# Attention over 32 heads: TensorE's program without its loop, and four steps of the other engines in another order

## The chip, the cores and the metric

One core of a Trainium2 chip runs the whole program. The metric is the device time of one execution in microseconds (us). The core has five engines with instruction queues of their own, which only semaphores bring together: TensorE (PE, with its weight loads PEld), VectorE (DVE), ScalarE (ACT), GpSimd (POOL) and SyncE (SP), which issues nearly all the DMA transfers of this part.

## What is computed

Two sequences of 2048 tokens of width 512 go through one decoder layer: self-attention with 16 heads of width 64 and a relative position bias, attention to a short context, and a feed-forward part in which 512 chosen tokens get a second, heavier network. The change touches the self-attention alone:

```python
q, k, v = (proj(Wq), proj(Wk), proj(Wv))
scores = jnp.einsum('bhqd,bhkd->bhqk', q, k)
bias = rel_bias[_relative_position_buckets(S)]
scores = scores + bias.transpose(2, 0, 1)[None]
attn = jax.nn.softmax(scores, axis=-1)
ctx = jnp.einsum('bhqk,bhkd->bhqd', attn, v)
```

## The kernel before

The 2 x 16 heads are numbered n = 0 to 31 and worked one after the other; `head(n, k, side)` exists on each engine (POOL, SP, PE, ACT, DVE) and `side` alternates between two sets of buffers. Heads -2 and -1 are only preparation. On PE, ACT, DVE and POOL the helper `heads` writes heads -2, -1, 0 and 29, 30, 31 out and runs heads 1 to 28 in a hardware loop (`Fori`) of 14 rounds with two heads each; SP has loops of its own.

Scores are kept transposed, with keys on the partitions. A head has 32 steps: `qb` (0 or 1) is the half of 1024 queries and `kt` (0 to 15) the tile of 128 keys. Two steps make a group, so a head has 16 groups g. In each group:

- PE (line 610, `largest`) computes two tiles of 128 queries by 512 keys for the row maxima, twice (`pair` 0 and 1), both times into the same two PSUM banks. DVE (line 939) reduces them to maxima. PE starts the next one only when DVE has finished the last (`max_done`). From group 3 on these maxima are those of head n+1.
- PE (line 629, `scores`) computes two steps of scores of head n from the operands in `stacks`. DVE (line 956, `near`) adds the bias near the diagonal, ACT (lines 814 and 817, `exp`) takes the exponential into `probs`, a ring of four steps, and POOL (line 354) adds it into `acc`.
- PE (line 641, `value`) multiplies the probabilities of the group before by V.
- In groups 2, 6, 10 and 14 PE also projects queries and keys of head n+2 (line 590, `project`, block tb = 0 to 3). ACT takes them out, and DVE makes the low parts: `queries_low` (962), `step` (969) in groups 3, 7, 11, 15, and `step_lo` (975) in groups 4, 8, 12 and in group 0 of the next head.

At the end of a half, `sum_of` (PE, line 651) adds up `acc` into PSUM bank PB, which it shares with the projection. ACT copies it to `sums` (`sums_out`, line 794). SP's `divisors` spreads it over partitions with four DMAs (line 431), DVE takes the reciprocal (`reciprocals`, line 982, placed by `RECIP_GROUPS`), and SP writes it to memory and reads it back broadcast (lines 436 and 439). POOL multiplies it in (`context`, line 329, placed by `CONTEXT_STEPS`), and SP's `store_ctx` (line 446) writes the result to memory.

SP works its queue in order. In head n it issues: `fill` of head n+1 (lines 416 to 425: copies of q and k into `stacks`, 12 transfers; it waits until all scores of head n-1 are done, because they read that side), V and bias of head n+1, the weights of head n+3, `guard(n, 1)` (lines 401 and 404: row maxima of the second half, through memory), `divisors(n-1, 1)` and `store_ctx(n-1, 1)`, `guard(n+1, 0)`, and last `divisors(n, 0)` and `store_ctx(n, 0)`. Where the batch changes (heads 13 and 14), `xn_block` reloads the normalized inputs in between.

Of the kernel before, what the change touches and what calls it, by code (L numbers as in the profile page):

```python
# [26 lines left out]
NH = NB * H  # L27
# [42 lines left out]
STEP_GROUPS = {4 * tb + 3: tb for tb in range(BLOCKS)}  # L70
LOW_GROUPS = {4 * (tb + 1) % GROUPS: tb for tb in range(BLOCKS)}
FIRST_MAX, LAST_MAX = 3, 2
SUM_GROUPS = {13: 0, 5: 1}
RECIP_GROUPS = {14: 0, 6: 1}
CONTEXT_STEPS = {31: 0, 15: 1}
PART = QW // P


# [88 lines left out]
def attention(nc, io, scr, homes):  # L167

    with ExitStack() as c:
# [109 lines left out]
        def heads(engine, head):  # L279

            head(-2, -1, 0)
            head(-1, -1, 1)
            head(0, 0, 0)
            with engine.Fori(0, NH // 2 - 2) as j:
                head(j * 2 + 1, j, 1)
                head(j * 2 + 2, j + 1, 0)
            for n in range(NH - 3, NH):
                head(n, n // 2, n % 2)
# [10 lines left out]
        def has_max(n, g):  # L299

            _, own, nxt, _ = parts(n)
            return own if g <= LAST_MAX else nxt
# [56 lines left out]
        def _(sp):  # L359
# [88 lines left out]
            def xn_block(tb, reload):  # L448

                if reload:  # L450
                    cols = slice(tb * 512, (tb + 1) * 512)
                    sp.wait_ge(s["proj"], 4 * H - BLOCKS + tb + 1)
                    sp.dma_start(xn_hi[:, :, cols].bitcast(F32), scr["xn"][0][:, :, cols]).then_inc(s["xn_ready"][tb], 16)
                    sp.dma_start(xn_lo[:, :, cols].bitcast(F32), scr["xn"][1][:, :, cols]).then_inc(s["xn_ready"][tb], 16)
                else:
                    sp.sem_inc(s["xn_ready"][tb], 32)

            def head(n, side, h_next=None, h_weights=None, reload=False):
                carry, own, nxt, prep = parts(n)

                early = isinstance(n, int) and n == -1
                if nxt:
                    fill(n + 1, 1 - side)
                if nxt and not early:
                    past(sp, s["pved"], n * STEPS)
                    sp.dma_start(v_head[:, 1 - side, :, :], scr_v[n + 1]).then_inc(s["v_in"][1 - side], 16)
                if nxt:
                    sp.dma_start(near_bias[:, 1 - side, :], scr["near"][h_next]).then_inc(s["near_in"][1 - side], 16)
                    sp.dma_start(far_bias[:, 1 - side, :], scr["rconst"][h_next].partition_broadcast(P)).then_inc(s["far_in"][1 - side], 16)
                if h_weights is not None:  # L470
                    sp.wait_ge(s["w_split"], n + 3)
                    sp.dma_start(w_in[:], io["wqk"][h_weights]).then_inc(s["w_in"], 16)
                    xn_block(0, reload)
                if isinstance(n, int) and n == NH - 1:
                    sp.wait_ge(s["scored"], (NH - 1) * STEPS)
                    sp.dma_start(enc, io["enc"].rearrange("b p k c -> p b k c")).then_inc(s["kv_in"], 16)
                    sp.dma_start(bk, io["bk"]).then_inc(s["kv_in"], 16)
                    sp.dma_start(bv, io["bv"].partition_broadcast(CL)).then_inc(s["kv_in"], 16)
                if own:
                    guard(n, side, 1)  # L480
                if carry:
                    divisors(n - 1, 1)
                    store_ctx(n - 1, 1)
                if isinstance(n, int) and n == NH - 2:
                    sp.wait_ge(s["proj"], 4 * NH)
                    sp.dma_start(wk2[:], io["wk2"]).then_inc(s["kv_in"], 16)
                    sp.dma_start(wv2[:], io["wv2"]).then_inc(s["kv_in"], 16)
                    sp.dma_start(wo[:], io["wo"]).then_inc(s["wo_in"], 16)
                if isinstance(n, int) and n == NH - 1:
                    sp.dma_start(bq[:], io["bq"]).then_inc(s["rows_in"], 16)  # L490
                    for t in range(2):
                        sp.dma_start(ctx[:, t, :, :], scr_rows[0, t]).then_inc(s["rows_in"], 16)
                        sp.dma_start(x[:, t, :], x_rows[t]).then_inc(s["rows_in"], 16)
                if h_weights is not None:
                    xn_block(1, reload)
                if nxt:
                    guard(n + 1, 1 - side, 0)
                if early:
                    for q in range(V_RING):
                        sp.wait_ge(s["vstored"][q], 16 * 2 * NT // V_RING)  # L500
                    sp.dma_start(v_head[:, 1 - side, :, :], scr_v[n + 1]).then_inc(s["v_in"][1 - side], 16)
                if h_weights is not None:
                    xn_block(2, reload)
                if own:
                    divisors(n, 0)
                    store_ctx(n, 0)
                if h_weights is not None:
                    xn_block(3, reload)
# [4 lines left out]
            with sp.Fori(0, H // 2 - 2) as j:  # L513
                n = j * 2 + 1
# [5 lines left out]
            with sp.Fori(0, H // 2 - 2) as j:  # L520
                n = j * 2 + H
# [17 lines left out]
        def _(pe):  # L539
# [36 lines left out]
            def project(m, tb, first, end):  # L576

                if first == 0:
                    if not (isinstance(m, int) and m == 0):
                        past(pe, s["step_lo"], 4 * m + tb)  # L580
                    if tb == 1:
                        past(pe, s["sum_out"], 2 * (m - 2))
                    if tb == 3:
                        past(pe, s["sum_out"], 2 * (m - 2) + 1)
                    if tb == 0:
                        pe.wait_ge(s["w_split"], m + 1)
                    pe.wait_ge(s["xn_ready"][tb], (m + 1) * 32)
                for a in range(first, end):
                    kk, wi, xi = TERMS[a]
                    mm = pe.matmul(ps[:, proj_bank(m, tb), :], w[wi][:, kk, :], xs[xi][:, kk, tb * 512:(tb + 1) * 512],  # L590
                                   start=a == 0, stop=a == len(TERMS) - 1)
                if end == len(TERMS):
                    mm.then_inc(s["proj"], 1)
# [131 lines left out]
                        if own if qb == 0 else carry:  # L725
                            sum_of(of, qb, 4 * (n + 2) + g // 4 if prep else 4 * NH)

            heads(pe, head)
            pe.wait_ge(s["exped"], NH * STEPS)
            for st in (STEPS - 2, STEPS - 1):  # L730
                value(NH - 1, None, 1, st)
# [149 lines left out]
        def _(dve):  # L881
# [143 lines left out]
            def head(n, k, side):  # L1025
                carry, own, nxt, prep = parts(n)
                if isinstance(n, int) and n == -2:
                    first_head()
                    return
                for g in range(GROUPS):  # L1030
                    lowered = None
                    if g in LOW_GROUPS:
                        tb = LOW_GROUPS[g]
                        if tb < BLOCKS - 1 and prep:
                            lowered = (n + 2, tb)
                        if tb == BLOCKS - 1 and own and nxt:
                            lowered = (n + 1, tb)
                    if has_max(n, g):
                        largest(n, side, g, 0)
                    if own:  # L1040
                        near(n, k, side, 2 * g)
                        near(n, k, side, 2 * g + 1)
                    if prep and g in STEP_GROUPS:
                        step(n + 2, STEP_GROUPS[g])
                    if lowered:
                        step_lo(*lowered)
                    if has_max(n, g):
                        largest(n, side, g, 1)
                    if prep and g in EVAC_GROUPS:
                        queries_low(n + 2, EVAC_GROUPS[g])  # L1050
                    if isinstance(n, int) and n == NH - 1:
                        if g == KEYS_GROUP - 1:
                            dve.wait_ge(s["scored"], (NH - 1) * STEPS)
                            dve.memset(k2[:], 0.0).then_inc(s["k2_zero"], 1)
                        if g == KEYS_GROUP:
                            keys_out(0)
                        if g == VALUES_GROUP:
                            key_values_out(0)
                    if g == FIRST_MAX + NT // 2 - 1 and nxt:
                        guards(n + 1, 0)  # L1060
                    if g == LAST_MAX and own:
                        guards(n, 1)
                    if g in RECIP_GROUPS:
                        qb = RECIP_GROUPS[g]
                        if own if qb == 0 else carry:
                            reciprocals(n if qb == 0 else n - 1, qb)
# [1367 lines left out]
```

## Time and profile before

| | before |
|---|---|
| time, median of 3 runs | 3970.04 us (3968.12 to 3971.11) |
| the profiled execution | 3972.34 us, span 3970.6 us |
| granted clock of TensorE, mean | 0.977 |
| busy: PE / POOL / DVE / ACT | 94% / 68% / 62% / 50% |

PE is the engine that is busy nearly always. PE's busy time is modelled and matmuls overlap, so the share alone says little: what counts is the regular distance between groups and where it is longer than the shortest. The self-attention heads fill the span from about 264 us to 2970 us; then come the context attention and the routed feed-forward.

### The profile page before, as it was taken

The numbers are of one execution on the slowest core, as the hardware profiler recorded it, in microseconds if no ns is written. First come the engines' busy times: TensorE is split into PE (matmuls) and PEld (weight loads), VectorE is DVE, ScalarE is ACT, GpSimd is POOL, SyncE is SP. The second block draws the span as 40 slices with busy tenths as digits, with TensorE's granted clock in tenths as the row PEclk, the third lists the DMA queues.
The fourth block names the chain that finished last, engine by engine and source line by source line (L and its number), as shares of the span: only waits on it lengthen the run. The fifth ranks groups of instructions, "written<-read, shape, count | busy, mean of one in ns | idle before, by whom it ended". The sixth has DMA issues, their size and how long they took to land. (4 is left out here: it accounts for less than half of the span.)

```text
span 3970.6 us, 64135 instructions
## 1 busy us (share of the span) xinstructions
PE 3727.9 (94%) x21277; PEld 2216.2 (56%) x21277; DVE 2466.4 (62%) x3356; ACT 2004.6 (50%) x3452; POOL 2681.1 (68%) x1402
## 2 busy tenths in 40 slices
PE   8989999999999989999999999999997999997899
PEld 7754444444444444444444444444446888885377
DVE  3466666666666656666666666666635777775632
ACT  3335555555555555555555555555553555553232
POOL 1128888888888878888988888889893343430010
PEclk9989999999999999999999999999998999998999
DMA  7652222432223452222332222332312333335710
GB/s 221 162 120 63 66 64 71 103 75 69 64 64 81 101 153 64 69 64 67 93 90 66 68 64 67 98 84 65 105 36 88 100 106 103 104 116 174 262 46 22
DMA packets 368370, 366.99 MB, mean 92 GB/s; under 512 B 189339, under 2 KB 261531, under 8 KB 362776
## 3 DMA queue, kind: packets, MB, share of 16 engines
q1 hardware_dynamic: 299064, 336.50, 31.6%
q10 hardware_dynamic: 67168, 20.98, 2.2%
q0 software_dynamic: 1920, 6.29, 0.5%
q8 instruction: 175, 2.87, 0.3%
q14 instruction: 43, 0.35, 0.0%
HBM read 142.64 MB, written 89.70 MB: 59 GB/s over the span
## 5 line engine op out<-in xcount | busy, mean ns | idle before, releaser
L354 POOL TENSOR_TENSOR acc<-acc,probs 128x1024 f32<-128x1024 f32 x894 | 2126.4, 2379 | 306.9 <-ACT probs L814 189.3
L939 DVE TENSOR_REDUCE maxes<-ps 128x2 f32<-128x1024 f32 x1024 | 1253.2, 1225 | 607.6 <-PE ps L610 596.7
L817 ACT ACTIVATE probs<-ps,far_bias 128x1024 f32<-128x1024 f32 (+7 forms) x1280 | 997.4, 819 | 795.4 <-DVE near_s L956 546.0
L641 PE MATMUL ps<-probs,v_head 128*64 128x512 f32 x4096 | 1002.1, 610 | 8.9 <-ACT ctx_out L800 6.9
L629 PE MATMUL ps<-stacks 64*128 64x512 f32 x6144 | 825.7, 398 | 1.8 <-ACT probs L814 1.8
L629 PEld LDWEIGHTS ps<-stacks 64*128 64x128 f32 x6144 | 591.0, 188 | 126.9 <-ACT probs L814 7.9
L610 PE MATMUL ps<-stacks 64*128 64x512 f32 x2048 | 508.0, 494 | 142.4 <-DVE maxes L939 56.9
L610 PEld LDWEIGHTS ps<-stacks 64*128 64x128 f32 x2048 | 194.5, 187 | 700.0 <-DVE maxes L939 464.3
L641 PEld LDWEIGHTS ps<-probs,v_head 128*64 128x64 f32 x4096 | 251.0, 137 | 463.0 <-issue 450.9
L956 DVE TENSOR_TENSOR near_s<-ps,near_bias 128x384 f32<-128x384 f32 (+2 forms) x576 | 265.8, 491 | 58.4 <-PE ps L629 55.3
L962 DVE TENSOR_TENSOR c_q<-ps,c_q 64x512 fp32r<-64x512 f32 x128 | 87.5, 684 | 311.2 <-ACT c_q L773 311.2
L814 ACT ACTIVATE probs<-near_s 128x384 f32<-128x384 f32 (+2 forms) x576 | 273.3, 475 | 0.0
L590 PE MATMUL ps<-xn_hi,w_hi 128*128 128x512 f32 x512 | 216.2, 422 | 0.0
L590 PE MATMUL ps<-xn_lo,w_hi 128*128 128x512 f32 x512 | 203.1, 397 | 0.0
L590 PE MATMUL ps<-xn_hi,w_lo 128*128 128x512 f32 x512 | 203.1, 397 | 0.0
L1283 POOL TENSOR_TENSOR m_rs<-m_rs,m_expo 128x1 f32<-128x1 f32 x32 | 17.5, 548 | 235.1 <-DVE m_rs L1527 235.1
L566 PE MATMUL ps<-stacks,xn_hi 128*128 128x512 f32 x512 | 164.9, 404 | 11.7 <-DVE xn_lo L908 9.6
L773 ACT CAST c_q<-ps 64x512 fp32r<-64x512 f32 x128 | 74.0, 578 | 184.1 <-PE ps L590 179.1
L351 POOL TENSOR_TENSOR acc<-probs 128x1024 f32<-128x1024 f32 x64 | 152.7, 2387 | 12.8 <-ACT probs L814 12.6
L1418 PEld LDWEIGHTS m_ps<-m_turned,both_wk 128*128 128x128 f32 x1024 | 122.6, 197 | 4.5 <-ACT m_turned L1476 2.0
L1418 PE MATMUL m_ps<-m_turned,both_wk 128*128 128x128 f32 x1024 | 123.2, 280 | 1.4 <-ACT m_turned L1476 1.4
L590 PEld LDWEIGHTS ps<-xn_hi,w_hi 128*128 128x128 f32 x512 | 96.5, 188 | 48.1 <-issue 30.4
(278 smaller groups left out, 4515.4 us busy)
## 6 DMA issues: line engine op xcount, KB each, us to landing
stacks<-c_q SPq DMA_DIRECT2D x128, 256.0 KB, 4.3
stacks<-c_d SPq DMA_DIRECT2D x64, 512.0 KB, 6.9
stacks<-c_k SPq DMA_DIRECT2D x32, 768.0 KB, 5.5
stacks<-c_k SPq DMA_DIRECT2D x64, 384.0 KB, 7.0
scr_v<-probs ACTq DMA_DIRECT2D x32, 512.0 KB, 4.1
v_head<-scr_v SPq DMA_DIRECT2D x32, 512.0 KB, 8.5
scr_ctx<-ctx_out SPq DMA_DIRECT2D x128, 128.0 KB, 2.3
both_ctx<-scr_ctx SPq DMA_DIRECT2D x32, 512.0 KB, 4.0
```

The source lines that it names most:

```text
L351: pool.tensor_tensor(acc[:, qb, :], probs[:, (st - 1) % PT_RING, :], pr, ALU.add).then_inc(s["summed"], 2)
L354: pool.tensor_tensor(acc[:, qb, :], acc[:, qb, :], pr, ALU.add).then_inc(s["summed"], 1)
L566: mm = pe.matmul(ps[:, value_bank(v), :], xs[i][:, k, t * P:(t + 1) * P], (wv_hi, wv_lo)[j][:, k, half * 512:(half + 1) * 512], start=at = ...
L590: mm = pe.matmul(ps[:, proj_bank(m, tb), :], w[wi][:, kk, :], xs[xi][:, kk, tb * 512:(tb + 1) * 512], start=a == 0, stop=a == len(TERMS) - 1)
L610: mm = pe.matmul(ps[:, max_bank(n, pair) + half, :], stacks[lane(half), mside, QS, q], stacks[lane(half), mside, KH[half], keys], start=Tr ...
L629: mm = pe.matmul(ps[:, bank + half, :], stacks[lane(half), side, of_keys[half], keys], stacks[lane(half), side, QS, of_queries], start=Fal ...
L641: mm = pe.matmul(ps[64 * half:64 * half + 64, PV, :], v_head[:, side, kt, :], probs[:, st % PT_RING, half * 512:(half + 1) * 512], start=k ...
L814: ins = act.activation(probs[:, st % PT_RING, a:z], near_s[:, st % 2, 0:z - a], ACT.Exp)
L817: ins = act.activation(probs[:, st % PT_RING, a:z], sc[:, a:z], ACT.Exp, bias=bias)
L939: dve.tensor_reduce(maxes[:, qt:qt + HALF_GROUPS // 2 + 1:HALF_GROUPS // 2, first_chunk + pair], ps[:, bank:bank + 2, :], AX.X, ALU.max).t ...
L956: dve.tensor_tensor(near_s[:, st % 2, 0:z - a], sc, near_bias[:, side, j0:j0 + z - a], ALU.add).then_inc(s["biased"], 1)
L1418: mm = pe.matmul(ps[:, Q2, m * P:(m + 1) * P], wq2[:, k, m * P:(m + 1) * P], turned1[:, k, :], start=k == 0, stop=k == KT - 1)
```

## The change

PE's program calls `head` for every n from -2 to 31 in Python, so that it has no loop; the other engines keep theirs. The sums of the two halves are taken in groups 9 and 1 (13 and 5 before), the reciprocals in groups 10 and 3 (14 and 6), the divisions on POOL at steps 25 and 11 (31 and 15). On SP `divisors(n, 0)` goes ahead of `guard(n + 1, ...)`. On DVE the second `largest` of a group goes ahead of `step` and `step_lo`. The projection's waits for the shared bank move with the sums.

```diff
-SUM_GROUPS = {13: 0, 5: 1}
-RECIP_GROUPS = {14: 0, 6: 1}
-CONTEXT_STEPS = {31: 0, 15: 1}
+SUM_GROUPS = {9: 0, 1: 1}
+RECIP_GROUPS = {10: 0, 3: 1}
+CONTEXT_STEPS = {25: 0, 11: 1}
@@ sync: head
                 if h_weights is not None:
                     xn_block(1, reload)
+                if own:
+                    divisors(n, 0)
                 if nxt:
                     guard(n + 1, 1 - side, 0)
...
                 if own:
-                    divisors(n, 0)
                     store_ctx(n, 0)
@@ tensor: project
-                    if tb == 1:
+                    if tb == 0:
                         past(pe, s["sum_out"], 2 * (m - 2))
-                    if tb == 3:
+                    if tb == 2:
                         past(pe, s["sum_out"], 2 * (m - 2) + 1)
@@ tensor
-            heads(pe, head)
+            for n in range(-2, NH):
+                head(n, n // 2, n % 2)
@@ vector: head
                     if own:
                         near(n, k, side, 2 * g)
                         near(n, k, side, 2 * g + 1)
+                    if has_max(n, g):
+                        largest(n, side, g, 1)
                     if prep and g in STEP_GROUPS:
                         step(n + 2, STEP_GROUPS[g])
                     if lowered:
                         step_lo(*lowered)
-                    if has_max(n, g):
-                        largest(n, side, g, 1)
```

## Rows read from the trace of the kernel before

**Rows 1.** The page, part 1: busy time of each engine.
```profile
PE 3727.9 (94%) x21277; PEld 2216.2 (56%) x21277; DVE 2466.4 (62%) x3356; ACT 2004.6 (50%) x3452; POOL 2681.1 (68%) x1402
```

**Rows 2.** Timeline (start us, us, what [idle before]): first scores of heads 1, 13, 15, 29.
```profile
349.20 0.86 PE L629 MATMUL ps<-stacks 64*128 64x512 f32 x6
...
1367.97 1.49 PE L629 MATMUL ps<-stacks 64*128 64x512 f32 x6
...
1548.38 1.27 PE L629 MATMUL ps<-stacks 64*128 64x512 f32 x6
...
2732.66 0.85 PE L629 MATMUL ps<-stacks 64*128 64x512 f32 x6
```

**Rows 3.** Waits of PE, whole span: us in total, times, longest us.
```profile
PE ps L610 <- DMA stacks<-c_k: 54.5, 23, 11.8
PE ps L610 <- issue: 28.6, 14, 2.3
```

**Rows 4.** Head 28: the group of line 610, then timeline of PE and DVE.
```profile
L610 PE MATMUL ps<-stacks 64*128 64x512 f32 x64 | 15.8, 489 | 3.9 <-DMA stacks<-c_k 1.9 <-DVE maxes L939 1.5 <-ACT probs L814 0.4
...
2651.22 0.68 DVE L975 TENSOR_TENSOR c_k<-ps,c_d 64x512 fp32r<-64x512 f32 x1
2651.94 1.23 DVE L939 TENSOR_REDUCE maxes<-ps 128x2 f32<-128x1024 f32 x1
2653.22 0.50 PE L610 MATMUL ps<-stacks 64*128 64x512 f32 x2 [0.52 <-DVE maxes L939]
...
2666.44 0.50 PE L610 MATMUL ps<-stacks 64*128 64x512 f32 x2 [1.93 <-DMA stacks<-c_k]
...
2671.05 0.50 PE L610 MATMUL ps<-stacks 64*128 64x512 f32 x2 [0.42 <-DVE maxes L939]
...
2672.87 0.50 PE L610 MATMUL ps<-stacks 64*128 64x512 f32 x2
...
2679.29 0.64 PE L651 MATMUL ps<-acc,ones 128*32 128x256 f32 x8
```

**Rows 5.** Timeline: last scores of head 27, first of head 28, SP's queue in head 28.
```profile
2643.86 1.54 PE L629 MATMUL ps<-stacks 64*128 64x512 f32 x12
...
2648.81 0.86 PE L629 MATMUL ps<-stacks 64*128 64x512 f32 x6
...
2650.72 1.25 SPq L446 DMA_DIRECT2D scr_ctx<-ctx_out  x2
2652.30 3.36 SPq L416 DMA_DIRECT2D stacks<-c_q  x4
...
2675.95 1.80 SPq L404 DMA_DIRECT2D guard_q<-scr_neg  x2
2680.39 2.51 SPq L431 DMA_DIRECT2D part<-sums  x4
```

**Rows 6.** Timeline of SP: the same two places in head 21, then in head 13.
```profile
2059.29 3.39 SPq L416 DMA_DIRECT2D stacks<-c_q  x4
...
2081.74 1.91 SPq L404 DMA_DIRECT2D guard_q<-scr_neg  x2
...
1369.89 3.36 SPq L416 DMA_DIRECT2D stacks<-c_q  x4
...
1398.84 1.96 SPq L404 DMA_DIRECT2D guard_q<-scr_neg  x2
```

**Rows 7.** The tile `part`: time from issue of line 431's DMAs to landing.
```profile
DMA to landing us min/median/max: 1.6/1.7/3.5
```

**Rows 8.** Head 30: timeline of PE behind a long wait, and the clock granted then.
```profile
2834.34 0.80 PE L610 MATMUL ps<-stacks 64*128 64x512 f32 x2 [5.13 <-DMA stacks<-c_k]
2834.91 2.79 PE L629 MATMUL ps<-stacks 64*128 64x512 f32 x12
...
2832.10:2838.80 6.70, 4.46 (x18) 2.98 (x20) 2.85 (x4) 1.67 (x3) 2.72 (x2) 0.50 1.02 238
...
2840.30 0.50 PE L610 MATMUL ps<-stacks 64*128 64x512 f32 x2
```

**Rows 9.** Timeline of POOL in head 28: nine steps in a row.
```profile
2669.99 22.56 POOL L354 TENSOR_TENSOR acc<-acc,probs 128x1024 f32<-128x1024 f32 x9 [3.14 <-ACT probs L814]
```

## The prediction

> **What bounds the kernel now.** I read the page's busy times first: PE is busy 94% of the span, no other engine over 68% [rows 1]. So a change pays where PE waits, and costs where it makes PE wait. Then I took the attention head by head, from the first scores of one head to those of the next [rows 2]: heads 1 to 12 take (1367.97 - 349.20) / 12 = 84.90 us each, heads 15 to 28 (2732.66 - 1548.38) / 14 = 84.59, the 26 together 84.73. Heads 13 and 14, with the reload, take 180.41 together. Third, the waits. Over the span PE waits 54.5 us for the transfers of `fill`, 23 times, and 28.6 us at the loop's branch, 14 times some 2.04 us [rows 3]. In one head, 28, it waits 3.9 us: 1.9 for `fill` and 2.0 for DVE and, once, ACT [rows 4]. That head and head 29, which is written out already, both take 83.85 us (2648.81 to 2732.66 for head 28 [rows 2, 5]), so it is my model of a head without a branch.
>
> Where the 2.0 us come from is seen at the end of group 0: DVE runs `step_lo` (0.68 us) ahead of the second reduction (1.23), and PE waits 0.52 us for that reduction before the next group; group 3 has the same with `step`, 0.42 us [rows 4]. The wait for `fill` comes from SP's queue: it issues `store_ctx(27, 0)`, which waits for POOL, at 2650.72, and only then the fill, at 2652.30 [rows 5], that is 3.5 us into head 28, although the scores it must wait for ended at 2643.86 + 1.54 = 2645.40, 3.4 us before the head began.
>
> **What the change gives.** *DVE's order.* The second reduction no longer stands behind `step` and `step_lo`; these fill time in which DVE would wait for the next maxima. Gain up to 1.9 us a head, and who needs their results (the fill's second part, ACT, the projection four groups on) is not at the limit. *The fill.* With the division at step 25, `store_ctx(n, 0)` is over before the head ends, and the fill starts when the last scores end: 3.0 us before the next head (2645.40 against a start moved 0.4 earlier, to 2648.4) instead of 3.5 after. Its operands land 6.5 us earlier, PE's need moves about 0.5; the 1.9 us are gone with 4 us to spare. *The loop.* The 2.04 us a round go, and nothing takes their place: head 29, written out, shows no issue wait. But the branch also gave the fill time, so it is no gain to be added to head 28's own: its rows already hold no branch. Without new waits a head would take 83.85 - 1.9 - 1.9 = 80.0 us, 4.7 less than the mean.
>
> The Trainium skill, Runtime: NRT & Kernel Launch, section Instruction fetch mechanics, says that a taken branch breaks the sequential prefetch, so that writing code out is to be preferred. By that rule the loop by itself is worth its whole 28.6 us; by the rows, writing it out alone would give 26 x (84.73 - 83.85) = 23, because a head without a branch meets the wait for the fill. The sum here is not made from either, but from a whole head.
>
> *What is moved at no cost.* The sums take 0.6 us of PE in either group [rows 4]; they need POOL's additions: those of steps 6 to 14 end 43.7 us into head 28 [rows 9], step 15 and the division add 3.8, and group 9, ten sixteenths of the head, ends after some 50. Were POOL later, PE would wait for the rest. The projection's waits for bank PB come a group after the sum; the scores of that group cover ACT's copy. `divisors(n, 0)`, seven transfers, goes past `guard(n + 1, 0)`, whose result is wanted only at the next head, over 20 us later.
>
> **What it costs.** `reciprocals(n-1, 1)` now stands at the end of group 3 in DVE's queue and waits there for the spread, line 431. Behind it stand the bias of step 8 and both reductions of group 4. Who waits for those is PE: the second `largest` of group 4 writes the banks that the first reduction must have read.
>
> When does DVE get there, and when does the spread land? Counted from the head's first scores. In head 28 the first `largest` of group 4, which follows DVE's last step of group 3, is at 2671.05, so 22.2 us in; without the waits of 0.5, 1.9 and 0.4 us and with a sum of 0.6 in group 1 that is 20.0. The second `largest` of group 4, now at 2672.87 or 24.1, would be due at 21.8 [rows 4, 5].
>
> The spread stands in SP's queue behind the whole fill, V, bias, weights, and `guard(n, 1)`. From the fill's first issue to the end of the guard's last issue head 28 takes 2675.95 + 1.80 - 2652.30 = 25.4 us [rows 5], head 21 24.4 [rows 6]; the rest of the loop's heads lie about there, since the guard's small write queues behind the fill's bytes. I take 24.9. Then four issues, of which the last starts 1.9 us after the first, and 1.7 us to its landing [rows 5, 7]: 3.6 us. With the fill starting at -3.0 the spread lands at -3.0 + 24.9 + 0.1 + 3.6 = 25.6. Today the sum comes so late that SP stands waiting for it (from 2677.75 to 2680.39 in head 28), and the reciprocal is due in group 6, after the landing.
>
> So DVE stands still from about 20.3 to 25.6. The reciprocal and hand-overs take about 0.3 (an estimate) and the first reduction 1.23: PE goes on at 27.1, 5.3 us late. The ctx store no longer shares the first microseconds with the fill: two transfers of 128 KB against some 1.15 us for each 256 KB one, so up to 1.2 us may come off. I take a wait of 5.0, between 4.1 and 6.0.
>
> *The clock.* Head 30 has such a wait today, 5.13 us. The granted clock is then 0.50 (1.2 GHz) from 2832.10 to 2838.80, and the group behind it takes 2840.30 - 2834.34 = 5.96 us, against 2671.05 - 2666.44 - 0.42 = 4.19 in head 28; the twelve scores alone take 2.79 against 1.54 [rows 4, 5, 8]. That is 1.8 us more. The bounds for the new wait: 0, if the clock stays at full speed as it does behind part of the 2 us waits, and 2.3, if 4.5 us of pure matmul run at half speed; I take 1.5, near the row of the same length. The Trainium skill, TensorE: Matmul & The Clock Gate, section HAM oscillation, says that a kernel that waits for a DMA in each tile starts each one at the slow clock. It speaks against this change: by it the 1.5 us come in all heads, without it the forecast would be 3981. Head 30 agrees, once.
>
> **The sum.** A head of 80.0 + 5.0 + 1.5 = 86.5 us. Against the 26 heads at 84.73 and head 29 at 83.85: 26 x 1.77 + 2.65 = +48.7. Head 13 reloads inputs ahead of the guard: 1398.84 + 1.96 - 1369.89 = 30.9 us instead of 24.9 [rows 6], so its wait is near 11 us and the head 92.8; head 14, 91 by the same reckoning (the reload now starts with the projection's end and no longer behind the store): 183.8 against 180.4, +3.4. Head 0 has no second half to divide: -2. Head 30 loses its 5.13 us and its slow clock, but gets to group 4 three microseconds sooner, without projection: +2. Head 31 is the same. Together +52 us. The profiled execution took 2.3 us more than the median, which doesn't matter for a difference: 3970.0 + 52 = 4022.
>
> **The rivals.**
> *The wait without the slow clock* (0.15): 85.0 a head, 26 x 0.27 + 1.2 + 3 = +11, so 3981. For it: behind many 2 us waits nothing is slow. Against it: head 30.
> *DVE's wait does not reach PE* (0.14): SP's transfers from fill to guard are the place. It decides in the time from first issue to the guard's end: at 22.7 us the spread lands at 23.4, the wait is about 3.2 and with 1.5 for the clock a head costs what it does now; at 18 us or less nothing is left of the wait. Then a head takes 80, not less, since POOL needs 22.56 / 9 = 2.51 us a step [rows 9], 75 for its 30 steps and four more for divisions and weights. 27 heads x 4.7 and some 20 us in heads 13 and 14: 3970 - 147 = 3823. For it: the lighter load on the queue. Against it: about 24 us in every head, and even with no backlog the guard would come after group 2.
> *The written-out code stalls* (0.05): if it had to be fetched like the branch's target, three blocks of about 2 us a head: 4022 + 180. Against it: head 29 takes what head 28 takes.
> *My forecast*: 0.66, 3985 to 4070 on its own.
>
> **How the numbers follow.** About 0.2% can be told from no change. Slower: 0.66 + 0.05 and half of the second case, 0.08: 0.79. Same: 0.07 of that case. Faster: 0.14. The range goes from 3965, with the case of the full clock and a wait of 4.5, to 4070, a wait of 6.0 and 2.2 for the clock.
>
> **What would show it.** In the changed trace DVE waits at line 982 in each head for the spread, some 5 us, and PE at line 610 in group 4 for DVE, about 5 us; no PE wait for `stacks<-c_k` and none on issue; groups 0, 3, 12 and 15 shorter by 0.4 to 0.5; heads of 86 to 87 us; more half-clock stretches behind group 4. If the spread lands before 22 us, or heads take 80 to 83 us, the prediction is wrong in the time of SP's queue; if the wait is there and heads take 85, it is wrong in the clock.

## The result, and the profile after

The changed kernel takes 4087.43 us (median of 4 runs, 4081.98 to 4094.89), against 3970.53 for the kernel before: a ratio of 1.0297, with a 95% interval of 1.0279 to 1.0315. It is 117 us slower. The forecast was 4022, 52 us slower, with a range of 3965 to 4070. So the sign and the mechanism came as forecast, and the size was less than half of what was measured, outside the range.

The profiled execution spans 4083.9 us. The page first: PE has 14 us more busy time than in [rows 1] and is busy 92% instead of 94% of a longer span, and DVE's work is 19 us less.

```profile
PE 3742.0 (92%) x21277; PEld 2211.3 (54%) x21277; DVE 2447.3 (60%) x3356; ACT 2015.9 (49%) x3452; POOL 2681.8 (66%) x1402
```

Then the waits (engine, tile, line, what it waited for: us in total, times, longest). First PE's largest, then its waits for the fill and at issue, then DVE's at the reciprocal.

```profile
PE ps L611 <- DVE maxes L941: 239.5, 39, 12.8
...
PE ps L611 <- DMA stacks<-c_k: 2.3, 2, 1.2
...
PE ps L611 <- issue: 0.8, 1, 0.8
...
DVE part_inv L984 <- DMA part<-sums: 248.2, 33, 12.9
```

These two answer [rows 3]. Both waits of before are as good as gone: `stacks<-c_k` has fallen from 54.5 us to 2.3 in 2 waits, and issue from 28.6 to 0.8 in 1. In their place stand 239.5 us for DVE, which itself stands 248.2 us at line 984 for the spread.

The head, which the prediction took as its model, is head 28 again. PE's timeline (start us, us, engine, line, what, idle before): the head's first scores, then all from the last scores of group 4 to the first `largest` of group 5.

```profile
2751.85 0.85 PE L630 MATMUL ps<-stacks 64*128 64x512 f32 x6
...
2771.90 1.56 PE L630 MATMUL ps<-stacks 64*128 64x512 f32 x12
2780.73 0.80 PE L611 MATMUL ps<-stacks 64*128 64x512 f32 x2 [7.26 <-DVE maxes L941]
2781.45 3.49 PE L642 MATMUL ps<-probs,v_head 128*64 128x512 f32 x8
2784.87 0.50 PE L611 MATMUL ps<-stacks 64*128 64x512 f32 x2
```

DVE in the same stretch: `step`, the reciprocal, and the reduction for which PE waits.

```profile
2771.16 0.70 DVE L971 TENSOR_TENSOR ps<-ps,c_d 64x512 f32<-64x512 f32 x1
2779.21 0.20 DVE L984 RECIPROCAL part_inv<-part 128x8 f32<-128x8 f32 x1 [7.35 <-DMA part<-sums]
2779.45 1.23 DVE L941 TENSOR_REDUCE maxes<-ps 128x2 f32<-128x1024 f32 x1
```

SP's queue in this head, where [rows 5] had the same lines, and below it how long the spread's small DMAs take from issue to landing, over the span (the answer to [rows 7]).

```profile
2749.07 3.36 SPq L416 DMA_DIRECT2D stacks<-c_q  x4
...
2772.68 1.88 SPq L404 DMA_DIRECT2D guard_q<-scr_neg  x2
2774.60 3.00 SPq L431 DMA_DIRECT2D part<-sums  x4
...
DMA to landing us min/median/max: 1.6/2.2/3.5
```

The fill starts 2.78 us ahead of the head (2749.07 against 2751.85), as foreseen. The spread's issue starts 22.75 us into the head and ends at 25.75, DVE takes up the reciprocal at 27.36, and PE goes on at 28.88, 7.26 us late. Behind the wait the eight matmuls of `value` take 3.49 us; elsewhere in the head they take 1.94. The clock granted in that stretch (us; PE, PEld, DVE, ACT, POOL busy and instructions; PEclk; DMA share; GB/s):

```profile
2779.00:2784.00 5.00, 3.27 (x8) 1.05 (x10) 3.53 (x5) 2.21 (x3) 1.81 (x1) 0.50 0.20 53
```

It is 1.2 GHz throughout these 5 us. Over the span the mean granted clock is 0.960, after 0.977 before. The trace's clock records have 42 stretches at half clock with 325 us together, against 31 with 181 us.

The mean over the heads 1 to 12 and 15 to 29 (first scores to first scores) is 88.99 us, against 84.70 in the same heads before. 27 x 4.29 = 116 us, which is the whole difference; heads 13 and 14 lose another 4 us, and head 0 gains as much. Group 4 takes 13.5 us of a head, where a group of its kind takes 4.12.

### The profile page after: what moved, and what is told of

It reads as the page before. It is cut to its first block and busy times, and to the rows that moved or that the text cites. A ratio compares the mean times of both kernels' runs of the same rounds, so it can differ in the third digit from the quotient of the medians.

```text
span 4083.9 us, 62609 instructions
## 1 busy us (share of the span) xinstructions
PE 3742.0 (92%) x21277; PEld 2211.3 (54%) x21277; DVE 2447.3 (60%) x3356; ACT 2015.9 (49%) x3452; POOL 2681.8 (66%) x1402
## 5 line engine op out<-in xcount | busy, mean ns | idle before, releaser
L642 PE MATMUL ps<-probs,v_head 128*64 128x512 f32 x4096 | 1040.8, 631 | 2.0 <-ACT probs L816 2.0
L611 PE MATMUL ps<-stacks 64*128 64x512 f32 x2048 | 513.8, 500 | 242.5 <-DVE maxes L941 239.5
L630 PEld LDWEIGHTS ps<-stacks 64*128 64x128 f32 x6144 | 582.4, 186 | 132.7 <-ACT probs L816 14.4
L611 PEld LDWEIGHTS ps<-stacks 64*128 64x128 f32 x2048 | 194.9, 187 | 809.0 <-DVE maxes L941 628.3
L958 DVE TENSOR_TENSOR near_s<-ps,near_bias 128x384 f32<-128x384 f32 (+2 forms) x576 | 264.5, 490 | 30.7 <-PE ps L630 28.6
L984 DVE RECIPROCAL part_inv<-part 128x8 f32<-128x8 f32 x63 | 12.5, 198 | 248.2 <-DMA part<-sums 248.2
```

The source lines that it names most:

```text
L611: mm = pe.matmul(ps[:, max_bank(n, pair) + half, :], stacks[lane(half), mside, QS, q], stacks[lane(half), mside, KH[half], keys], start=Tr ...
L630: mm = pe.matmul(ps[:, bank + half, :], stacks[lane(half), side, of_keys[half], keys], stacks[lane(half), side, QS, of_queries], start=Fal ...
L642: mm = pe.matmul(ps[64 * half:64 * half + 64, PV, :], v_head[:, side, kt, :], probs[:, st % PT_RING, half * 512:(half + 1) * 512], start=k ...
L958: dve.tensor_tensor(near_s[:, st % 2, 0:z - a], sc, near_bias[:, side, j0:j0 + z - a], ALU.add).then_inc(s["biased"], 1)
```

## The experiments

My theory: the second half's reciprocal, now in group 3, waits for a spread that cannot land before some 26 us, and PE pays for that wait and for the slow clock behind it. The rivals were that the time comes from the written-out program, from the fill that now lies differently in DMA, or from DVE's order. Each run changes one of these. "Heads" below is always the mean of the same 27 heads.

**Where the reciprocal stands: groups 4, 5 and 6.** For groups 5 and 6 the division on POOL (`context`), which needs the reciprocal's result, is moved with it, to steps 13 and 15; for group 4 it stays at step 11. The edit for group 5:

```
-RECIP_GROUPS = {10: 0, 3: 1}
-CONTEXT_STEPS = {25: 0, 11: 1}
+RECIP_GROUPS = {10: 0, 5: 1}
+CONTEXT_STEPS = {25: 0, 13: 1}
```

> The changed kernel with the reciprocal of the second half back in group 6 and its division back at step 15; everything else of the change stays. Theory (PE waits in group 4 for DVE, which waits in group 3 for the spread): DVE no longer waits at the reciprocal, PE's wait of 7.4 us and the slow clock of 2.0 us behind it are gone, a head takes 88.99 - 9.4 = 79.6 us, the total is about 3805 us. Rival (the loss comes from the written-out program or from the earlier fill, and DVE's wait only hides in it): over 3970 us. Rival (POOL becomes the bound): heads of 81 to 82 us, 3850 us.

> The changed kernel with the reciprocal of the second half one group later, in group 4. Theory: the spread lands at the same time, DVE gets to it one group of 4.1 us later, so PE's wait is about 3.3 us and the slow clock costs about 1.5: 84.4 us a head, about 3955 us. If the wait did not scale with the place of the reciprocal (rival: something else in group 4), the time would stay near 4087.

> The changed kernel with the reciprocal of the second half in group 5 and its division at step 13. Theory: DVE gets to the reciprocal at about 28 us, after the spread's landing at 27 in most heads, and the context's store is over before ACT needs its tile in group 8, so the 1.2 us that TensorE waits for it in group 9 with the reciprocal in group 6 go too: heads of 79.6, 3805 to 3820 us. Rival: with the reciprocal so near the landing, every head whose spread is late (up to 29 us) waits again: 3840 us or more.

Group 6: 3836.74 us, ratio 0.9663 (0.9647 to 0.9679), heads 80.70. Group 4: 3942.07 us, 0.9924 (0.9908 to 0.9941), heads 84.28. Group 5: 3808.24 us, 0.9583 (0.9567 to 0.9599), heads 79.62. DVE's wait in the run with group 4, both waits in the run with group 5, and the largest wait of PE in the run with group 6:

```profile
DVE part_inv L984 <- DMA part<-sums: 122.4, 33, 9.3
```
```profile
PE ps L611 <- DVE maxes L941: 20.8, 16, 4.9
DVE part_inv L984 <- DMA part<-sums: 31.1, 13, 9.4
```
```profile
PE ps L642 <- ACT ctx_out L802: 36.6, 31, 3.9
```

One group later takes half of DVE's wait away (248.2 to 122.4 us), and the long group moves with the reciprocal: group 5 takes 8.75 us, and group 4 is back at 4.12. Two groups later the wait is gone in all but a few heads. So the wait is for a landing at a fixed time, not for something the reciprocal does; and 279 us (4087 to 3808) hang on the place of one reciprocal and the division that goes with it. The program without its loop, the earlier fill and DVE's order are all still in the run with group 5, so none of them is what makes the change slow. With group 6 the expectation missed by 30 us. There the division comes so late that the values of the next half wait in group 9 until ACT has emptied their bank into `ctx_out`; that group takes 5.86 us instead of 4.69: 27 x 1.17 = 32 us.

**Where the spread stands in SP's queue.** The spread of the second half is issued ahead of the guard, whose second part waits for a landing; once with the reciprocal in group 3 as in the change, once with it in group 5 (and the division at step 13).

```
+                if carry:
+                    divisors(n - 1, 1)
                 if own:
                     guard(n, side, 1)
                 if carry:
-                    divisors(n - 1, 1)
                     store_ctx(n - 1, 1)
```

> The changed kernel with the second half's division put ahead of the guard in SP's queue; the reciprocal stays in group 3. Theory (the spread is late because of its place in SP's queue): it is issued about 16.4 us into the head instead of 22.8 and lands near 22 us, behind the fill's bytes, DVE waits about 2 us, heads of 82 us, about 3890 us. Rival (the spread's landing is bound by the bytes ahead of it alone, whatever its place): the landing stays at 26 to 27 us and the time over 4050 us.

> After with both mends at once: the second half's reciprocal in group 5 and ctx_out at step 13, and on SP the spread of the second half's sums ahead of the second half's guard rows. With the reciprocal in group 5 alone VectorE still waited in the few heads whose spread landed late (heads 2, 12, 13, 14 and 22, up to 8 us). My theory (the spread's landing is the only thing left that is late): with the spread some 5 us earlier in the queue these waits go, heads 79.5 us throughout except head 13 (the reload of xn, which holds the spread's transfers), 3790 to 3805 us. Rival (the guard rows behind the spread become late for the second half's scores, or the heads' floor is PE's own work): no gain, 3805 to 3815 us.

With group 3: 3858.7 us, 0.9721 (0.9705 to 0.9738), heads 81.32. With group 5: 3802.77 us, 0.9579 (0.9563 to 0.9595), heads 79.67. DVE's wait in the first, and two of PE's waits in the second:

```profile
DVE part_inv L985 <- DMA part<-sums: 63.8, 32, 9.3
```
```profile
PE ps L612 <- DVE maxes L942: 10.7, 9, 3.2
...
PE ps L628 <- DMA guard_q<-scr_neg: 8.2, 8, 4.6
```

Moving the spread forward takes away three quarters of the wait with the reciprocal where the change put it. That shows the other side of the same race: DVE's place and SP's place decide together. The expected 3890 was too high: the spread lands 20.4 to 23.3 us into the head. With group 5 it only helps heads 13 and 14, with the reload (161.1 us together against 169.1), and costs a little in eight heads, where the guard now lands late. It is 4.2% under the kernel before and 7% under the changed one; its 5 us, or 0.14%, against the run with group 5 alone are too little to tell the two apart.

**What the slow clock costs.** PE gets matmuls to do where it stands still in group 4. The output stays the same, since they add zeros to the running sum of the values. First small ones, then full ones, of the size of the projection's:

```
+                    if own and carry and g == 4:
+                        for _ in range(60):
+                            pe.matmul(ps[0:64, PV, 0:P], guard_keys[32:64, 0, 0:64].bitcast(F32), ident[32:64, :],
+                                      start=False, stop=False, skip_group_check=True)
```
```
+                    if own and carry and g == 4 and n not in (13, 14) and n < 29:
+                        for _ in range(26):
+                            pe.matmul(ps[:, PV, :], zt[:], xn_hi[:, 0, 1536:2048],
+                                      start=False, stop=False, skip_group_check=True)
```

> The changed kernel with 60 small matmuls ahead of TensorE's wait in group 4, which add zeros to the context's bank: TensorE works where it stood still. It does more work than the kernel needs, nothing is left out. Theory (2.0 us a head behind the wait are the slow clock): the granted clock stays at 1.0 through group 4, heads of 87.0 instead of 89.0 us, about 4030 us. Rival (group 5 is slow because DVE catches up): 4080 us or more.

> After, with 26 more matmuls (a zero 128x128 tile against 512 columns of xn_hi, added to the running sum of the values, so nothing changes) where TensorE waits in group 4 of heads 1 to 28, save 13 and 14. At full clock each takes some 0.235 us, together 6.1 us, less than the wait of 7.3 us. Theory (the slow clock behind the wait comes from TensorE's standing still): granted clock 1.00 behind the wait, group 4 without the 2.0 us it lost, heads 87.0 us, total 4030 to 4045 us. Rival (the slow clock comes of something else than the wait, or the added matmuls bring it themselves, as the small ones did): 4080 us or more, half clock within the added matmuls.

Small: 4508.5 us, ratio 1.1354. Full: 4038.47 us, 1.0178 (1.0161 to 1.0195), heads 87.06. PE's timeline in head 28 of the first, with the granted clock (the number ahead of the DMA share: 1.00, 0.52, 0.50) in three stretches while the added matmuls run:

```profile
3129.37 20.32 PE L707 MATMUL ps<-ident,guard_keys 32*64 32x128 f32 x120
...
3131.00:3135.00 4.00, 4.00 (x39) 4.00 (x38) 0.00 (x0) 0.00 (x0) 0.85 (x1) 1.00 0.16 2
3135.00:3139.00 4.00, 4.00 (x22) 4.00 (x21) 1.62 (x3) 1.36 (x3) 0.08 (x1) 0.52 0.03 3
3139.00:3143.00 4.00, 4.00 (x21) 4.00 (x20) 0.00 (x0) 0.85 (x1) 3.86 (x2) 0.50 0.18 64
```

The same place with the full ones, and the clock in the 5 us that follow:

```profile
2727.98 6.33 PE L709 MATMUL ps<-xn_hi,zt 128*128 128x512 f32 x26
2735.39 0.50 PE L613 MATMUL ps<-stacks 64*128 64x512 f32 x2 [1.08 <-DVE maxes L947]
2735.82 1.94 PE L644 MATMUL ps<-probs,v_head 128*64 128x512 f32 x8
...
2734.00:2739.00 5.00, 3.92 (x24) 1.76 (x24) 4.18 (x6) 2.29 (x4) 2.15 (x1) 1.00 0.22 57
```

The first is a failed test: the small matmuls took 20.32 us instead of filling a gap of 7, and the granted clock fell to 0.50 while they ran, so the run says nothing of the wait. The second is the test that was wanted. DVE's wait is as long as in the change (244.3 us in all, against 248.2), PE is busy in it, the granted clock stays at 2.4 GHz, and `value` takes its 1.94 us. Heads take 87.06 instead of 88.99 us. The slow clock is thus worth 1.93 us a head (head 29, one of the 27, has no added matmuls), and 49 us of the total; the wait itself is the rest.

**The parts alone.** The change with the loop of TensorE's program put back; the kernel before with TensorE's program written out and nothing else; the kernel before with DVE's new order and nothing else.

```
-            for n in range(-2, NH):
-                head(n, n // 2, n % 2)
+            heads(pe, head)
```
```
-            heads(pe, head)
+            for n in range(-2, NH):
+                head(n, n // 2, n % 2)
```
```
+                    if has_max(n, g):
+                        largest(n, side, g, 1)
                     if prep and g in STEP_GROUPS:
                         step(n + 2, STEP_GROUPS[g])
                     if lowered:
                         step_lo(*lowered)
-                    if has_max(n, g):
-                        largest(n, side, g, 1)
```

> The whole change, but with TensorE's loop kept. Theory A (a fetch of TensorE's code that falls into the fill delays it by 2 to 4 us, and the loop keeps the fetches out of that stretch): the spread lands at 24.8 us after the fill's start in each head, as in the kernel before, no heads of 90 us or more between others of 88.5; against that 13 branches of 2.0 us, in part with the slow clock: 4085 to 4110 us. Theory B (the spread's late landing has nothing to do with the code's fetches): the same scatter of 24.4 to 27.6 us as in the changed kernel, 4115 us or more.

> The kernel before with only TensorE's program written out. Theory: the 2.04 us at each branch go, the fill's wait takes a part of it back, heads of 83.85 us instead of 84.73: 3947 us. Rival (the written-out code costs time by itself, in fetching): 3970 us or more, with issue waits on PE in each head.

> The kernel before with only VectorE's order changed (second reduction ahead of step and step_lo). Theory: PE's waits for DVE at the ends of groups 0, 3, 12 and 15 go, some 1.9 us a head; the 0.9 us of groups 0 and 3 come back as a longer wait for the fill in the heads that wait for it. Between 1.0 and 1.9 us a head, 30 heads: 3915 to 3940 us. Rival (the order gives nothing, since PE is not held by the reduction): 3970 us.

The change with the loop: 4105.72 us, 1.0336 (1.0319 to 1.0353), heads 89.43. Writing out alone: 4009.45 us, 1.0096 (1.0080 to 1.0113), heads 85.86. DVE's order alone: 3945.8 us, 0.9925 (0.9908 to 0.9942), heads 84.15. PE's largest waits in the first; in the second, followed by group 2's end in its head 28 and in its head 10; in the third.

```profile
PE ps L611 <- DVE maxes L940: 214.8, 38, 11.2
PE ps L611 <- issue: 22.0, 13, 2.1
```
```profile
PE ps L610 <- issue: 95.9, 29, 13.2
...
2698.46 0.50 PE L610 MATMUL ps<-stacks 64*128 64x512 f32 x2 [2.25 <-issue]
2698.77 2.31 PE L629 MATMUL ps<-stacks 64*128 64x512 f32 x12
...
1141.26 0.79 PE L610 MATMUL ps<-stacks 64*128 64x512 f32 x2 [5.04 <-issue]
```
```profile
PE ps L610 <- DMA stacks<-c_k: 72.8, 23, 14.0
PE ps L610 <- issue: 30.2, 14, 2.7
```

Taking the loop out is not what makes the change slow: with the loop the kernel is slower still. Writing out is worth 18 us inside the change (4106 to 4087). The run with the loop came out within the range of its theory A, but not by that theory: the loop does not keep the fetches out of the fill. The last section has what they do there.

Alone, in the kernel before, writing out costs 39 us. That was a miss of 62 us, 3947 against 4009. The time is the rival's, 3970 or more with issue waits in each head, but not its reason, and the rows tell why. The 29 waits that the view puts down to issue are no branches (there is none left). Each of them ends 0.09 us after the last `c_k` rows have landed; in head 28 the landing is at 17.9 us and PE goes on at 18.0. In the loop, a head that comes right behind a branch waits for its fill 1.1 us at most, since the branch gave the fill time, and each other one (head 14 aside) 1.9 to 2.5. Written out, all wait. By groups, in the mean of the 27 heads, a head gains 0.81 us in its last group, where the branch was, and 0.25 in its first; it loses 1.63 in group 2 to the wait for the fill, and 0.56 in group 3 to the slow clock. That clock follows the wait in nearly every head: 2.31 us for twelve scores that take 1.56 at full clock. Seven heads, 5, 10, 15, 18, 20, 25 and 30, wait 4.5 to 7.9 us (head 10, shown, 5.04), the others (head 14 aside) 1.8 to 2.8. In the seven the last `c_k` rows land 16.1 to 18.6 us after the fill's first issue, elsewhere (heads 0 and 14 aside) 14.0 to 14.4.

DVE's order alone gives 25 us of the 51 that 1.9 us a head would be, a little less than expected (3946 us, not 3915 to 3940). Its waits at the ends of groups are gone (group 12 takes 4.12 us, 4.72 before); PE meets the fill that much sooner, and the wait for it grows from 54.5 [rows 3] to 72.8.

**Why the fill is late in seven heads.** In these heads the trace has a packet of 16 KB in queue q8 (of kind "instruction") 5 to 10 us after the fill's first issue; in the others (head 0 aside, with one at 12) there is none between 0 and 16 us. Over five heads the packets number 18, so they fall at other places in each head. To test it, TensorE's program is made four such blocks long in each head: written out as above, plus 102 increments of a semaphore for which nobody waits, and in a second run 128 more in head 0, so that all that follows lies half a block earlier. Below, `range(32)` is the second run's; the first has `range(0)`.

```
                     mm = pe.matmul(ps[:, proj_bank(m, tb), :], w[wi][:, kk, :], xs[xi][:, kk, tb * 512:(tb + 1) * 512],
                                    start=a == 0, stop=a == len(TERMS) - 1)
+                    if 3 <= m <= NH - 1 and a + 1 < end:
+                        for _ in range(2):
+                            pe.sem_inc(s["pad"][m % 3], 1)
                 if end == len(TERMS):
                     mm.then_inc(s["proj"], 1)
+                    if 3 <= m:
+                        for _ in range(4 if tb < 2 else 3):
+                            pe.sem_inc(s["pad"][m % 3], 1)
+                    if m == 2:
+                        for _ in range(32):
+                            pe.sem_inc(s["pad"][m % 3], 1)
```

> Before with TensorE's program written out, and 102 increments of a semaphore that nobody waits for in each of heads 1 to 29 of TensorE's program, so that a head is some 1024 instructions, four whole blocks of 16 KB code. The code's fetches then fall at the same place of every head: from head 1 of the written-out kernel, whose fetch was 21.9 us into the head, at some 19.5 us, 16 us after the fill's first issue, and again some 1 us ahead of the next head's start. Theory (a code fetch between 0 and 14 us after the fill's first issue delays the fill): the last k row lands 14.1 to 14.3 us after the fill's first issue in every head but 14, heads 85.1 us, total 3985 to 3995 us, under the 4009 of writing out alone. Rival (the late fills of heads 5, 10, 15, 18, 20, 25 and 30 have another cause): they stay late, 4009 us or more.

> The same with 128 more increments in head 0, so that all later fetches lie half a block earlier: at some 9 us into each head, 5 us after the fill's first issue. Theory: the last k row lands 16 to 18.5 us after the first issue in every head, TensorE waits for it 2 to 4 us longer in group 2 of every head, heads 88 to 89 us, total 4070 to 4095 us, some 90 us above the run with the other phase. Rival (the fetch's place does not matter): the two runs agree within 10 us.

The first: 4006.35 us, 1.0088 (1.0072 to 1.0105), heads 85.97. The second: 4145.37 us, 1.0449 (1.0431 to 1.0467), heads 89.77. The queues of DMA in head 28 of the second, 7.4 to 11.4 us into the head (queue, kind: packets, MB, share of 16 engines), and PE's wait for the fill in it:

```profile
q1 hardware_dynamic: 387, 1.15, 97.8%
q8 instruction: 1, 0.02, 1.5%
...
2806.31 0.50 PE L620 MATMUL ps<-stacks 64*128 64x512 f32 x2 [4.34 <-issue]
...
PE ps L620 <- issue: 132.9, 29, 12.4
```

The first, with its one packet 21 to 24 us into the head, behind the fill:

```profile
q8 instruction: 1, 0.02, 2.4%
...
2700.98 0.49 PE L620 MATMUL ps<-stacks 64*128 64x512 f32 x2 [1.59 <-issue]
...
PE ps L620 <- issue: 61.1, 29, 13.6
```

That q8 carries TensorE's code is seen in the pages: its packets number 151 in the written-out kernel and 163 in both padded ones, 12 more for 2958 added increments. In the first run the packet lies 17.0 to 20.0 us after the fill's first issue, and the last `c_k` rows land 14.1 to 14.4 us after it, in every head from 1 on but 14. In the second it lies 1.4 to 5.5 us after, and they land 15.7 to 18.1 us after it, again in every head from 1 on but 14. The instructions of a head are the same, only their place against the blocks differs: 3.8 us a head in the profiled executions (the second's is the fastest of four, which go from 4118 to 4154 us). So one packet of code in that stretch of the fill delays it by 1.5 to 4 us; that is shown. Both totals missed, the first by some 15 us (3985 to 3995 expected), the second by 50 (4070 to 4095). One reason is that the increments are not free: groups 6, 10 and 14, with the projections, take 7.11 us without them and 7.58 to 7.74 with them. What else the second run lost is open.

## Why the prediction was wrong, and where it was right

**What it named came.** DVE waits at the reciprocal, PE in group 4 for DVE, the slow clock follows, and the waits for `c_k` and for the branch are gone. Heads 13 and 14 take 184.3 us together (183.8 forecast), head 0 80.8 (2 less forecast, 4 less measured), head 30 80.0 against 79.7 (forecast 2 more). The base is right too: a head without the new wait and its clock takes 88.99 - 7.4 - 2.0 = 79.6 us, forecast 80.0, and the run with the reciprocal in group 5 takes 79.62.

**The step that failed is the size of PE's wait: 7.4 us, not 5.0.** 2.4 us in 27 heads are 65 us, all that is missing between 4022 and 4087; the other differences (the clock, the base, heads 0, 13, 14 and 30) cancel. In head 28, term by term: the fill starts at -2.78 (forecast -3.0); from its first issue to the end of the guard's 25.49 (24.9; mean of the 27 heads 25.45); the spread from its first issue to landing 4.5 (3.6). It lands at 27.3, not at 25.6. The largest part, 0.9, was in the spread itself. I took its 2.51 us of issue and 1.7 of landing from [rows 5, 7], where SP had stood idle ahead of it, so that its four DMAs met an empty queue. Right behind the guard the same four take 3.00 to issue and a median of 2.2 to land. A row that could have warned me existed. In head 13 of before, SP had not stood idle ahead of the spread: it took 3.07 us to issue, and 4.26 from first issue to last landing.

```profile
1398.84 1.96 SPq L404 DMA_DIRECT2D guard_q<-scr_neg  x2
1400.84 3.07 SPq L431 DMA_DIRECT2D part<-sums  x4
```

Next, 0.6 of the stretch from fill to guard. In the ten heads of the change (of 1 to 12 and 15 to 28) whose fill meets no packet of code in its first 14 us, the stretch is 24.8 us in the mean, as forecast and as in the kernel before (24.9). In the other sixteen it is 25.8, and up to 27.6; in head 28 a packet comes at 11.2 us. No head of the kernel before that I read the stretch from had such a packet, so it could not show this. The rest is small: PE was due at 21.6, not at 21.8, took 0.1 longer from the landing on, and I had taken 0.3 off the wait for a lighter queue, which the stretch does not bear out.

**The clock** was 2.0 us and not 1.5 (1.93 by the run with the full matmuls): 27 x 0.5 = 14 us more, and the base, 0.4 lower, gives 11 back. I had placed it near the row of the same length, head 30, but below it (1.8 there), as a middle between it and nothing; the row itself would have been the better forecast. The Trainium skill, TensorE: Matmul & The Clock Gate, section HAM oscillation, was weighed there as speaking against the change. The trace agrees in each of the 27 heads, with a granted clock of 0.50 to 0.62 in the 4 us behind the wait, and the run with the full matmuls, in which PE does not stand still, has the clock at 1.00 behind the same wait of DVE.

**What the loop is worth** was wrong though it was no term of the sum. I took 23 us off for writing out alone, with head 29, which is written out in the kernel before, as a head that shows no issue wait. The measured effect is 39 us more. And head 29 does show one. It is the fourteenth of [rows 3], and no branch: it ends 0.09 us after the landing of the last `c_k` rows, like those of the written-out kernel.

```profile
2750.29 0.50 PE L610 MATMUL ps<-stacks 64*128 64x512 f32 x2 [1.91 <-issue]
```

So the loop has 13 branches with 26.7 us. What writing out puts in their place, a wait for the fill in every head, stood in this row; the slow clock behind it did not. The Trainium skill, Runtime: NRT & Kernel Launch, section Instruction fetch mechanics, prefers code that is written out. By that rule the 26.7 us would be won; here the measurement decides against it, in the kernel before. Inside the change the measurement goes the rule's way: with the loop PE stands 22 us at branches, and without it the kernel is 18 us faster.

**The rivals.** The wait without the slow clock, 3981: no, the clock is slow in each head. DVE's wait not reaching PE, 3823: no, but the distance was small, as its decision point said. Two groups later it does not, and 3808 is measured. The written-out code stalls: not by its own fetch, PE's issue waits are 0.8 us in all. The fetch did cost time, by way of the fill, which was in none of my cases.

## What to carry to other kernels

A step with a wait that is put into an engine's queue holds up all that stands behind it. So compare the earliest landing of what it waits for with the time at which the engine gets there, head by head, and move it behind the landing and no further: here the place of one reciprocal is worth 279 us, and one group too far costs 28 again. Durations of small DMAs must come from a row in which the queue ahead of them is as full as it will be, not from one that stood idle. And a wait that is taken away at one place comes back at the next late thing, so the price of a branch or of a wait is read from a run with that part alone, not from its row.

## What the runs showed of the hardware

A fetch of 16 KB of TensorE's code delays the kernel's own transfers; the profile counts both among the packets of the same 16 DMA engines. In all fourteen kernels traced, and in every head but 14 (the reload) and 29, the last rows of a fill land 14.0 to 14.5 us after its first issue where no such packet falls into the first 14 us, and 14.7 to 19.0 us after it where one does, though the packet itself takes only 0.9 to 1.8 us. The latest landings, 17 to 19, belong to packets within 7 us after the first issue; those at 11 us cost 0.5 to 2.2. In head 29 of the changed kernel there are packets of 8 KB of a second instruction queue instead (q14): three of them 5 to 10 us after the first issue, and the rows land after 16.6 us. A single one of these, at 9.4 us in head 16, does not show: the rows land after 14.4. Why so small a packet costs so much isn't settled. In heads 1 to 30 of the kernel before no 16 KB packet falls into those 14 us: with the loop the fetches lie near the same places in each round. Written out, with 18 blocks in five heads, they wander through the fill. With the loop kept, but the fill starting earlier, the refetch at the branch falls into it in each second head, and there its last rows land after 17.2 to 19.0 us.

A stretch of 120 matmul records of 32 rows by 64 columns on 128 columns ran with TensorE busy in the whole stretch. The granted clock fell from 1.00 to 0.50 within it, and came back while the larger matmuls behind it ran. 26 matmuls of 128x128 on 512 columns in the same place kept it at 1.00. Which property of the two makes the difference wasn't tried.
